# A four-layer Flamingo block: routed experts computed per sorted block of 128 tokens instead of densely

## What is computed

```python
logits = xf @ gate_w.T + lb_bias
scores = jax.nn.sigmoid(logits)
topw, topi = jax.lax.top_k(scores, 2)
topw = topw / (topw.sum(-1, keepdims=True) + 1e-08)
for e in range(8):
    m = topi == e
    sel = m.any(axis=-1)
    wmean = (topw * m).sum() / jnp.maximum(m.sum(), 1)
    y = silu(xf @ gw[e].T) * (xf @ uw[e].T) @ dw[e].T      # inner width 128
    out = out + jnp.where(sel[:, None], y * wmean, 0)
out = out + mlp(x, shared_gate_w, shared_up_w, shared_down_w)   # inner width 256
```

## Time and profile before

| | us |
|---|---|
| median of three runs | 718.27 (716.75 to 718.84) |
| the profiled execution | 717.3 |
| its span | 715.0 |
| experts stage within the span | 293.4 to 494.0 |

### The profile page before, as it was taken

One profiled execution on the slowest core, in us unless ns is written; L12 is line 12 of the kernel. 1 busy time (PEld: TensorE's weight loads), 2 busy tenths in 40 slices (PEclk: granted clock), 3 DMA queues, 4 the chain that ended last, 5 costly groups with the idle time before them and its releaser, 6 DMA issues. The chain is left out here.

```text
span 715.0 us, 9809 instructions
## 1 busy us (share of the span) xinstructions
PE 646.9 (90%) x3329; PEld 410.1 (57%) x3348; DVE 459.5 (64%) x778; ACT 343.2 (48%) x598; POOL 311.7 (44%) x482
## 2 busy tenths in 40 slices
PE   5996999999999988989999999997889989976885
PEld 3563343434434247656777777775558676853553
DVE  4878788888888137487343433436284757479894
ACT  3545588888888853454222222432412212014564
POOL 9767657686444306600010000101041727186796
PEclk9997699999999979999999999998999999998999
DMA  8769935747400058002100000001000000000011
GB/s 274 189 229 276 191 51 67 91 53 90 47 1 1 1 201 329 16 0 83 50 1 1 0 0 0 1 0 60 0 1 1 0 1 0 1 1 8 30 35 46
DMA packets 23143, 43.40 MB, mean 61 GB/s; under 512 B 4060, under 2 KB 10848, under 8 KB 22336
## 3 DMA queue, kind: packets, MB, share of 16 engines
q1 hardware_dynamic: 15224, 31.02, 13.1%
q0 software_dynamic: 6048, 10.03, 10.8%
q10 hardware_dynamic: 1832, 1.84, 1.2%
HBM read 32.27 MB, written 10.49 MB: 60 GB/s over the span
## 5 line engine op out<-in xcount | busy, mean ns | idle before, releaser
L744 DVE TENSOR_REDUCE mx<-ps_f 128x2 f32<-128x1024 f32 x128 | 148.8, 1218 | 27.1 <-PE ps_f L660 25.9
L847 ACT ACTIVATE prob<-ps_s 128x512 f32<-128x512 f32 x256 | 135.7, 605 | 28.7 <-PE ps_s L678 16.8
L678 PE MATMUL ps_s<-q_stacks,k_stacks 53*128 53x512 f32 x256 | 90.5, 455 | 1.1 <-ACT prob L847 1.1
L678 PEld LDWEIGHTS ps_s<-q_stacks,k_stacks 53*128 53x128 f32 x256 | 41.3, 190 | 60.0 <-ACT prob L847 39.6
L660 PE MATMUL ps_f<-k_stacks,q_stacks 53*128 53x512 f32 x256 | 65.4, 478 | 7.2 <-DVE mx L744 5.0
L687 PE MATMUL ps_o<-prob,vst 128*32 128x512 f32 x512 | 70.7, 627 | 1.2 <-ACT prob L847 0.9
L180 POOL TENSOR_TENSOR norm_tmp_att<-st 128x4 f32<-128x4 f32 x4 | 1.0, 241 | 145.4 <-DVE st L1371 145.4
L1332 DVE SCALAR_TENSOR_TENSOR h<-ps_u,most,qs 128x512 f32<-128x512 f32 x32 | 24.0, 750 | 62.7 <-ACT qs L1262 62.7
L1262 ACT ACTIVATE qs<-ps_g 128x512 f32<-128x512 f32 x40 | 23.9, 597 | 82.5 <-PE ps_u L1133 82.5
L771 POOL TENSOR_TENSOR q_stacks<-minus,q_stacks 128x1024 fp32r<-128x1024 f32 x16 | 38.0, 2377 | 33.7 <-ACT minus L838 31.8
L660 PEld LDWEIGHTS ps_f<-k_stacks,q_stacks 53*128 53x128 f32 x256 | 29.1, 197 | 32.8 <-DVE mx L744 29.0
(11 more groups left out here) (305 smaller groups left out, 1452.4 us busy)
## 6 DMA issues: line engine op xcount, KB each, us to landing
k_stacks<-room_k POOLq DMA_DIRECT2D x18, 256.0 KB, 6.0
q_stacks<-room_q POOLq DMA_DIRECT2D x18, 256.0 KB, 5.3
up<-in_up SPq DMA_DIRECT2D x10, 256.0 KB, 6.3
x<-in_x SPq DMA_DIRECT2D x4, 512.0 KB, 9.4
ctx_raw<-in_ctxTC SPq DMA_DIRECT2D x4, 512.0 KB, 7.4
room_k<-k_high SPq DMA_DIRECT2D x4, 512.0 KB, 4.7
room_k<-k_low SPq DMA_DIRECT2D x4, 512.0 KB, 6.3
room_q<-q_high SPq DMA_DIRECT2D x4, 512.0 KB, 5.5
```

What stands on the lines that cost most here:

```text
L678: pe.matmul(ps_s[n % 3][:, :], ks[rows(h), 2 * s + pair, kt * P:(kt + 1) * P], qs[rows(h), 2 * s + pair, :], start=True, stop=True).then_i ...
L744: dve.tensor_reduce(mx[:, f % 2, qt, 2 * pair:2 * pair + 2], ps_f[n % 2][:, :, :], AX_X, ALU.max).then_inc(used, 1)
L847: act.activation(prob[:, kt % 2, j, :], ps_s[n % 3][:, :], ACT.Exp, scale=SCALE)\
```

## The change

- In attend, SP fills the HBM buffer `sorted_x` with zeros by nine DMAs of 2 MB, one for each step of `lowered` from the sixth on; POOL makes the tile of zeros.
- In experts, only the two shared units of each batch stay dense (m = 0 to 7; 18 matmuls each, no mask and no weight). The first four run ahead of the routed work, the last four behind it.
- DVE turns the ranks into a row number of each token in each chosen expert's region of `sorted_x` (PE counts the tokens ahead with small bf16 matmuls, `places`), a table of 40 block numbers and experts (`block_table`), and the way back (`back_rows`).
- POOL scatters the normed tokens to HBM: 32 indirect DMAs of 128 rows of 1 KB.
- SP and PE read the table into 40 registers each. Then 20 pairs of blocks of 128 tokens run: SP loads a pair (two DMAs with an address from a register, four pairs in flight), PE turns it (4 transposes), ACT and DVE split it, PE makes gate and up side by side (12 matmuls of 256 columns, the expert's weights as the moving operand by register), silu, product, 2 transposes, split, 6 matmuls of 256 columns, a copy, and two stores to `sorted_y`. 20 pairs run whatever the choice of the tokens.
- SP loads wg and wu only when all pairs are done; ACT waits for them ahead of the last four shared units.
- POOL waits for all stores and gathers each token's two rows back: 32 indirect DMAs, eight for each batch. Those of batch 2 and 3 wait until DVE has combined batch 0 and 1, as the four batches share 8 tiles; the statistics of an earlier batch stand between them. DVE adds the rows to x with their weights (`combine`), and then takes the statistics.
- Semaphores of the earlier stages are cleared by SP so that they can be used again.

```diff
+            cleared = cleared.rearrange("n p (r s) -> n p r s", s=S)
+            sp.wait_ge(zeroed, 1)
+            for i in range(E + 1):
+                sp.wait_ge(lowered, 6 + i)
+                sp.dma_start(cleared[i], zeros[:, :].rearrange("p (o s) -> p o s", o=1)
+                             .broadcast_to([P, REGION * D // (P * S), S])).then_inc(room_clear, 16)
...
+            for old in used_up:
+                sp.sem_clear(old)
...
+            sp.wait_ge(table_ready, 1)
+            at = [sp.value_load(table_i[0:1, 1, j:j + 1], min_val=0, max_val=ROWS_ALL // BLOCK - 1) for j in range(BLOCKS)]
...
+            sp.wait_ge(xsplit, B)
+            sp.wait_ge(scattered, 16 * 2 * T)
+            for j in range(4):
+                load(j)
+            for j in range(PAIRS):
+                if j + 4 < PAIRS:
+                    load(j + 4)
+                if j:
+                    store(j - 1)
+            store(PAIRS - 1)
+            sp.wait_ge(pair_done, PAIRS)
+            for i, n in ((0, "wg"), (1, "wu")):
+                sp.dma_start(w32[i], a[n]).then_inc(w32_in, 16)
...
+            for half in range(2):
+                pool.wait_ge(row_ready, half + 1)
+                for t in range(8 * half, 8 * half + 8):
+                    for c in range(2):
+                        pool.indirect_dma_start(sorted_x, offset(row_i, c, t), norm["tile"](t), None).then_inc(scattered, 16)
+            pool.wait_ge(back_ready, 1)
+            for i in range(3):
+                pool.wait_ge(block_out[i], 32 * ((PAIRS - 1 - i) // 3 + 1))
+            for b in range(B):
+                if b > 1:
+                    pool.wait_ge(combined, 2 * (b - 1))
+                for t in range(b * QT, (b + 1) * QT):
+                    for c in range(2):
+                        pool.indirect_dma_start(own["back"][t % (T // 2)][:, c, :], None, sorted_y, offset(back_i, c, t))\
+                            .then_inc(gathered[b], 16)
+                if b > 1:
+                    batch_statistics(pool, per, next_norm, b - 2)
+            batch_statistics(pool, per, next_norm, B - 2)
...
+            def block_pair(j):
+                u = j % 2
+                at = lambda w, q, d: w[:, ds(expert[2 * j + q], 1), :, d, :].rearrange("p o i n -> p (o i) n")
+                terms = [(own["x_high"], w_high), (own["x_high"], up_low), (own["x_low"], w_high)]
+                pe.wait_ge(top_done, j + 1)
+                pe.wait_ge(low_done, j + 1)
...
+            expert = [pe.value_load(table_i[0:1, 0, j:j + 1], min_val=0, max_val=E - 1) for j in range(BLOCKS)]
+            pe.wait_ge(y_used, 2 * FRONT)
+            pe.wait_ge(wsplit, NX)
+            pe.wait_ge(dsplit, 3)
+            block_turned(0)
+            block_turned(1)
+            for j in range(PAIRS):
+                block_pair(j)
+                if j + 2 < PAIRS:
+                    block_turned(j + 2)
+                if j:
+                    block_rows(j - 1)
+                block_h_turned(j)
+            block_rows(PAIRS - 1)
+            pe.wait_ge(rows_kept, PAIRS)
+            for m in range(SH * FRONT, SH * B):
+                gate_up(m)
...
+            keep_y(FRONT - 1)
+            choice_weights()
+            back_rows()
+            residual(FRONT - 1)
+            for k in range(SH * FRONT - 1, NX):
+                low_w(k)
+            low_d(1, 0, E // 2)
             low_d(2, E // 2, E)
+            low_x(3)
+            block_low(0)
+            block_low(1)
+            for j in range(PAIRS):
+                block_hidden(j)
+                if j + 2 < PAIRS:
+                    block_low(j + 2)
+                block_low_h(j)
+            for m in range(SH * FRONT, SH * B):
+                hidden(m)
...
+            combine(0)
+            combine(1)
             keep_y(B - 1)
             residual(B - 1)
+            combine(2)
+            combine(3)
```

More of the change, by code:

```diff
@@ L22 @@
 BF16 = mybir.dt.bfloat16
+I32 = mybir.dt.int32
 F16 = mybir.dt.float16
@@ new lines, in store @@
+            def store(j):
+                sp.wait_ge(rows_kept, j + 1)
+                for q in range(2):
+                    sp.dma_start(y_blocks[2 * j + q], own["y"][j % 3][:, q, :])\
+                      .then_inc(block_out[j % 3], 16)
+            sp.wait_ge(xsplit, B)
[7 more added lines that the diff above has]
+                    store(j - 1)
@@ new lines, in block_h_turned, with block_rows @@
+            def block_h_turned(j):
+                pe.wait_ge(own_h, j + 1)
+                for q in range(2):
+                    last = pe.transpose(ps_hidden[j % 2][:, q * P:(q + 1) * P], own["h32"][:, j % 2, q, :], id32)
+                last.then_inc(own_turned, 1)
+            def block_rows(j):
+                u = j % 2
+                at = lambda w, q: w[:, ds(expert[2 * j + q], 1), :].rearrange("p o d -> p (o d)")
+                wait(pe, rows_kept, j - 1)
+                terms = [(own["high"], d_high), (own["high"], down_low), (own["low"], d_high)]
+                pe.wait_ge(own_high, j + 1)
+                pe.wait_ge(own_low, j + 1)
+                for q in range(2):
+                    for n, (h, w) in enumerate(terms):
+                        last = pe.matmul(ps_rows[u][:, q, :], h[:, u, q * P:(q + 1) * P], at(w, q), start=(n == 0),
+                                         stop=(n == 2))
+                last.then_inc(rows_done, 1)
@@ new lines, in choice_weights @@
+            def choice_weights():
+                link(dve.tensor_scalar(most[:, 0, :], most[:, 2, :], per["gates"][:, 2:3], None, ALU.mult))
+                share = most[:, 0, :].rearrange("p (o e) -> p o e", o=1).broadcast_to([P, T, E])
+                for c in range(2):
+                    last = dve.tensor_tensor(picked[:, c, :, :], pick[:, c, :, :], share, ALU.mult)
+                link(last)
+                link(dve.tensor_reduce(weights[:, :, :], picked[:, :, :, :], AX_X, ALU.add))
@@ L1425, in _ @@
             low_w(1)
[L1426 to L1428 removed]
+            ranks(0)
+            logit_half(1)
             low_d(0, E, NX)
[L1430 to L1439 removed]
+            rows(0)
+            ranks(1)
+            hidden(0)
+            low_h(0)
+            rows(1)
+            low_x(1)
+            hidden(1)
             chosen = both[:, 1, :, :].rearrange("p e t -> p t e")
```

615 lines of the change are left out of this document (366 added, 249 removed).

## The result

The changed kernel takes 724.96 us (median of 4, 723.49 to 727.45) against 718.56 us beside it: ratio 1.0083, 95% interval 1.0042 to 1.0124. Two later series beside the kernel before gave 1.0052 (1.0015 to 1.0089) and 1.0028 (0.9988 to 1.0067). So it is slower by 0.3 to 0.8% (the last interval reaches no change), where 708 us was forecast. The profiled execution took 723.5 us with a span of 721.5; the one of before 717.3 and 715.0.

What follows compares the result with a forecast made beforehand. It took TensorE alone to bound the experts' stage. From 717.3 us profiled it took 10.6 for the next block starting earlier and added 1.0, giving 707.7, forecast as 708 with a range of 690 to 745.

Steps and rivals of the forecast that it cites:

- pair 0: Start of the first pair of blocks in the experts' stage, forecast at 358.5 us, the latest of four candidates counting.
- What goes: Experts' stage: 32 of 40 dense units, the routed experts, go at 4.38 us each, 140 us of PE.
- (c): Ahead of the first pair: PE's 40 register loads in series, 0.3 us each, hidden; showing above 0.34 each.
- rival (3): Ahead of the pairs: register loads cost 0.6 us each, first pair at 369, +10, 718 us; chance 0.08.
- (a): Ahead of the first pair: DVE's front, table at 335, DVE ready at 357, first pair starting at 358.5.
- (b): Ahead of the first pair: POOL's 32 serial scatters, 1.1 us each, done by 354.4, hidden up to 1.23 each.
- rival (1): Scatters and gathers: indirect DMAs are dear and POOL bounds, deciding from 1.43 us each; 755 at 2.0; chance 0.20.
- Pair loop: The 20 pairs of blocks: PE 2.92 us a pair, 3.2 with 0.3 added, 64 us in all.
- The wait I feared: Within a pair, PE's wait for silu and the product: 1.1 us behind 1.2 of cover, so 0.3 was added.
- The wait for wg and wu: Behind the pairs, ACT waits for wg and wu, issued late: 7.0 us to land, showing by 2.7.
- The gathers: Stage's end: POOL's gathers at 1.1 us each, batch 2's waiting for combine(0); next block at 483.4, not 494.0.
- rival (4): In attend: the nine clearing DMAs hold up attention by 10 us, 717 us; chance 0.05.

Runs made afterwards that it cites:

- loads_two: The changed kernel with PE's 40 one-register loads of the table made two loads of 20 registers: 714.61 us, ratio 0.9947 to the kernel before.
- four: The changed kernel with PE's and SP's table loads by 20, later ScalarE passes over wg and wu, and POOL's statistics moved: 701.32 us, 0.9755.
- one_choice_again: Repeat of the changed kernel with PE's loads by 20 and the scatters of every token's second choice left out: 714.42 us, 0.9944.
- pair_two_terms: The changed kernel without the third term of gate and up in the pairs, 8 matmuls instead of 12: 714.81 us, 0.9930.

## Why the prediction was wrong, point by point

Measured 723.5 us in the profiled execution against 707.7 summed: 15.8 us. They split as follows, in times of the stage with the 2.6 us taken off by which it began later:

| step | forecast | measured | difference |
|---|---|---|---|
| pair 0 | 358.5 | 370.2 | +11.7 |
| pair 0 to rows_kept(last) | 69.5 | 61.2 | -8.3 |
| from there to VectorE free | 22 | 26.8 | +4.8 |
| VectorE free to the last statistics | 33.2 | 33.7 | +0.5 |
| from there to the next block | 0.2 | 5.75 | +5.5 |
| stages ahead | +1 | +2.6 | +1.6 |

The last row is within the spread between profiles and says nothing of the forecast.

**What goes.** The 32 units went as costed. PE's busy time in the stage fell from 193.6 to 126.1 us, by 67 (over the whole span by 64.7), where 140 less 57 of pairs would be 83; the stretches at a clock of 0.50 (446 to 451 above is one) are part of the rest, and how much of it was not traced.

**Pair 0: the step that failed, (c).** The prediction took 0.3 us for a register load, between 0 and a small DMA's round trip, with the threshold at 0.34 beside it. It is 0.65 to 0.67, PE is idle for 25 us, and rival (3) happened, to which I gave 0.08: it had 0.6 us, pair 0 at 369 (370.2 measured) and 718. The value taken lay on the cheap side of a threshold that nothing in the trace supported. The Trainium skill (Runtime: NRT & Kernel Launch, Instruction fetch mechanics) has some 200 ns a register, told of loads from HBM; the TENSOR_LOAD alone, from SBUF, was 301 here, and a checked load is three instructions, 650 together. Loads of 20 registers removed 5.6 us, and doubling the loads added 25.9.

The 11.7 us of the table can be split by the experiments. From the first scatter to the first gate matmul of pair 0 the forecast had 46.5 us (312 to 358.5), and the changed kernel took 58.2. With PE's loads short (loads_two) it is 52.6, and with SP's short too (four) 49.3. So PE's loads made 5.6 of it, SP's loads behind them 3.3, and the scatters the last 2.8.

**What I had not costed at all: SP's 40 loads.** The change has them in plain sight. They take 24 us from the table's readiness, 336 to 360.6, and set SP's first tile load to the microsecond. In the changed kernel they were hidden behind PE's; in one_choice_again they held the loop while neither scatters nor VectorE did, and shortening them brought it 4.0 us forward. The table came at 333.4 in the times of the table above (forecast 335), and VectorE's front ended at 352.1 (forecast 357), so (a) was 5 us too long.

**Scatters, (b), and rival (1).** Priced at 1.1, measured 1.27 to 1.33, above the 1.23 at which they were to show. They did not, because the register loads were later; in four, where the loads are short, they set pair 0. By the prediction's own sum, 1.33 a scatter gives 361.8 for pair 0, 49.8 us after the first scatter; four has 49.3. The scatters stayed below the 1.43 from which rival (1) decides, so that rival did not happen.

**Pair loop.** Right in mechanism: PE 40.00 of 40.00 us. 2.92 was summed from 256-column matmuls scaled by their columns, 2.83 measured, so the added 0.3 was not there. The wait I feared stays 0.2 us behind PE, as pair_two_terms showed. Likewise the 3.5 us for the tail chain and the 2 us of clock were near: 372.8 + 20 x 2.83 = 429.4, and rows_kept(last) at 434.0, 4.6 us.

**Behind the loop.** The wait for wg and wu was seen, and undersized: 2.7 forecast, 4.3 of PE's idle time measured, since wu landed in 8.3 us, not 7.0. Missed was what the pause does: PE comes back at a granted clock of 0.50 for 5 us (446 to 451), and work that takes 5 us at half clock takes 2.5 at full, so another 2.5 us. Moving ScalarE's passes brought the stage's end 5.4 us forward. That the same wait also held POOL (through combine(0)) was in the sum as an order, but not as a thing to be removed.

**The gathers.** The tail's mechanism was right and its size too: 33.7 against 33.2 us. A gather was dearer (1.25 against 1.1, on the 16 of batches 2 and 3 +2.4), combine and landing cheaper by nearly as much.

**The barrier.** Nothing was put down for POOL's drain; the earlier trace rows showed 0.2 us, but of a block in which POOL issued no DMA. It cost 5.5 us. A figure for it stood in the same trace: attend's drain outlasts POOL's last instruction by 4.0 us with 48 plain DMAs, 83 ns each, and 64 x 83 ns is 5.3.

**Clears, rival (4).** Right: nothing that shows, against 1 us put down.

Taken together, the forecast was short by four costs on sequencers and at the barrier (PE's loads, ScalarE's wait with its clock, the drain, SP's loads behind them), none of which an engine's busy time shows, and by the scatters behind them; the pair loop gave 8.3 us back. Removing most of the four gave 701.3 us, 6 less than the 707.7 that were forecast. The gain of the change itself is small for the reason that the sum had in it. 140 us of PE went. In their place PE waits 25.1 us ahead of the pairs, takes 64.0 from its first own tiles to the last four shared units, waits 4.3 among these, and from its last shared unit to the next block another 38.7 us pass (461.6 to 500.3), in which it has only its last 8 transposes and 18 small matmuls. The 64 indirect DMAs are 32 x 1.33 + 32 x 1.29 = 84 us in series on POOL; most of the scatters and the gathers of batches 0 and 1 run beside PE's shared units, the others do not.

## What to carry to other kernels

Here a checked register load cost 0.56 to 0.67 us, one after the other, on each of the two engines that read the table. Count the loads on all of them, and load many with one instruction. Before a step that turns a wide, dense computation into a sorted one, count the instructions that issue the indirect DMAs: each cost 1.25 to 1.33 us here, with only 0.07 less for 64 rows instead of 128, and they stand in series on POOL. Look at the end of a block too: POOL's drain grew with the DMAs that it had issued, and a drain off the path in one stage shows what it costs in another. Where a removed wait brings less than its size, look for the next one in the trace before naming it: here it was a queue that the forecast had left out.

## What the runs showed of the hardware

- A checked register load from SBUF: 0.65 to 0.67 us on PE (301 + 146 + 18 ns and gaps), 0.62 on SP, and 0.56 on SP with half the scatters (one_choice_again). Twenty in one instruction: 1.4 to 1.7 us, and 0.3 for the range steps of each, 14.8 us for 40 on PE and 13.3 on SP.
- An indirect DMA of 128 rows of 1 KB on POOL: 0.95 to 0.97 us and 0.30 before the next; mean steps 1.29 (gather) and 1.33 (scatter). With 64 rows, measured on the scatters, 0.07 us less.
- POOL's drain at a block's end took 5.289 us with 64 indirect DMAs issued in the block, and 3.982 with 48, so 83 ns for each. In the same stage of the kernel before, without any, it took 0.04; in its attend, with 48 plain ones, 4.776, of which 4.0 behind POOL's last instruction.
- In one series, all three kernels with scatters had a stretch of 5 to 27 us, from 18 us after the first scatter until 2 to 6 us after the end of the last, in which ScalarE stood still; in the two where SP was reading its table then, it took about 1.4 us an instruction. The same kernels in other series had none of it. What sets it off stays open.
